# A tail of attention moved into the steps of an LSTM loop, on one NeuronCore

## The reference

```
x_proj = einsum('btd,gd->btg', x, W_ih) + b_ih + b_hh
def step(carry, xp):                       # 6250 steps, one after the other
    h, c = carry
    i, f, g, o = split(xp + h @ W_hh.T, 4)
    c = sigmoid(f) * c + sigmoid(i) * tanh(g)
    h = sigmoid(o) * tanh(c)
lstm_out = h of all steps
logits = einsum('bth,lh->btl', lstm_out, W_lin) + b_lin     # 2 classes
g = argmax(logits)                                          # 0 or 1 for each time step
w = g * lstm_out
inc = cumsum(w, axis=time);  prefix = inc - w;  suffix = inc[last] - inc
return 2.0 * lstm_out + prefix * fw_att + suffix * bw_att
x = x + that
```

## Time and profile before

| | |
|---|---|
| median of 3 runs | 13971.03 us |
| the profiled execution's own time | 13987.69 us |
| its span | 13985.9 us |
| PE, DVE, ACT busy, share of the span | 72%, 62%, 37% |
| DVE, fin of the recurrence | 13822.7 us |

### The profile page before, as it was taken

The page is one execution under the profiler, slowest core; times in us unless marked ns, Lnnn a source line. Parts: engine busy times, 40 slices in busy tenths (PEclk is TensorE's granted clock), DMA queues, the critical chain, the costliest instruction groups (busy, mean ns, idle before and its releaser), DMA issues. The chain is left out here.

```text
span 13985.9 us, 721250 instructions
## 1 busy us (share of the span) xinstructions
PE 10063.6 (72%) x285273; PEld 9131.5 (65%) x285273; DVE 8604.1 (62%) x65379; ACT 5184.4 (37%) x32393; POOL 2070.5 (15%) x1598
## 2 busy tenths in 40 slices
PE   3444444687777777777777777777777777777776
PEld 2333333567777777777777777777777777777775
DVE  4444222256666666666666666666666666666667
ACT  1111111144444444444444444444444444444443
POOL 5888788400000000000000000000000000000000
PEclk8666777865555555555555555555555555555556
DMA  6555455410000000000000000000000000000001
GB/s 164 91 90 90 80 83 83 92 34 1 1 1 1 1 1 1 1 1 1 1 1 1 1 1 1 1 1 1 1 1 1 1 1 1 1 1 1 1 1 19
DMA packets 2057504, 301.47 MB, mean 22 GB/s; under 512 B 1894943, under 2 KB 2013747, under 8 KB 2056843
## 3 DMA queue, kind: packets, MB, share of 16 engines
q0 software_dynamic: 150048, 204.90, 9.0%
q1 hardware_dynamic: 1896678, 91.09, 8.1%
q10 hardware_dynamic: 10742, 5.06, 0.1%
HBM read 153.07 MB, written 141.27 MB: 21 GB/s over the span
## 5 line engine op out<-in xcount | busy, mean ns | idle before, releaser
L1422 PE MATMUL bank<-hp,whh 128*128 128x1 f16 (+1 forms) x225000 | 7000.0, 166 | 2320.7 <-DVE hp L1553 2320.7
L1422 PEld LDWEIGHTS bank<-hp,whh 128*128 128x128 f16 x225000 | 6488.6, 104 | 2864.1 <-DVE hp L1553 2863.6
L1500 ACT ACTIVATE gates<-last_banks 128x3 f32<-128x3 f32 x12500 | 2085.4, 174 | 6161.2 <-DVE last_banks L1538 6161.2
L1538 DVE TENSOR_REDUCE last_banks<-bank 128x3 f32<-128x6 f32 x12500 | 2076.6, 172 | 2393.9 <-PE bank L1422 2393.9
L1422 PE MATMUL bank<-xsteps,wih 128*128 128x10 f16 (+1 forms) x45036 | 2331.0, 170 | 0.0
L1542 DVE CUSTOM_DVE_ANT_1 uv<-gates 128x4 f32<-128x4 f32 x12500 | 2019.4, 164 | 506.3 <-ACT gates L1500 0.2
L1553 DVE TENSOR_TENSOR_SCAN hp<-last_banks,opening 128x2 f16<-128x2 f32 x12500 | 1968.9, 161 | 569.1 <-ACT last_banks L1509 108.7
L1509 ACT ACTIVATE last_banks<-gates 128x1 f32<-128x1 f32 x12500 | 2085.2, 174 | 0.1
L1422 PEld LDWEIGHTS bank<-xsteps,wih 128*128 128x128 f16 x45036 | 1917.6, 104 | 0.0
L1558 DVE TENSOR_TENSOR_SCAN hp<-last_banks,hp 128x2 f16<-128x2 f32 x12500 | 1759.2, 159 | 0.0
L1629 POOL TENSOR_TENSOR U<-U (+1 forms) x25 | 27.5, 1139 | 11171.2 <-POOLq L1572 11171.2
(11 more groups left out here) (184 smaller groups left out, 3199.8 us busy)
## 6 DMA issues: line engine op xcount, KB each, us to landing
xsteps<-x_d SPq DMA_DIRECT2D x1252, 5.0 KB, 1.8
U<-hp SPq DMA_DIRECT2D x1250, 5.0 KB, 2.5
acc_d<-zero SPq DMA_DIRECT2D x30, 640.0 KB, 12.9
ht<-acc_d SPq DMA_DIRECT2D x75, 224.0 KB
rows<-xn_d,staged_i POOLq DMA_INDIRECT x782
acc_d<-sums,target POOLq DMA_INDIRECT x782, 3.8
xi<-xn_d SPq DMA_DIRECT2D x50, 125.0 KB
xi<-in_x SPq DMA_DIRECT2D x50, 125.0 KB
```

Of the source, the lines that this page charges most:

```text
L1422: return nc.tensor.matmul(to, w, v, start=start, stop=True, skip_group_check=True)
L1500: nc.scalar.activation(gates[:, k, 0:6:2], zi[k], ACT.Tanh, scale=down)\
L1538: nc.vector.tensor_reduce(zi[k], gi[k][b][:, s], axis=AX.X, op=ALU.add).then_inc(ifg_summed[k], 1)
```

## The change

All of the attention that doesn't need the last sum is done within the recurrence, ten time steps at a time, one iteration behind. DVE gets, behind `state2` of each step, a piece of it (`join` and `follow`): step 0 joins the second half of the ten states just finished, step 1 adds twice the states to `XT`, step 3 makes the gate, step 4 weighs, step 5 joins the first half of the running iteration's states, steps 6 and 7 do the running sum of the halves `k` = 0, 1, and steps 8 and 9 add to `XT`, for `k` = 0 and 1, first the weighted states times `minus_fw`, then the running sum times `diff`; the second of the two waits on the first, through the semaphore `after`. PE gets, in steps 1 and 2, behind the step's products, two float32 matmuls each (`class_logits`: 128x128 weights `wlb`, 10 columns), and its 44 ahead matmuls are shared out anew (`share`: 12, 3, 3, 12, 14, for both groups). ACT adds the bias to the first logit at the end of step 2. The stores of the states into `U` go, with their waits. Weights and constants are loaded and made in the block before the recurrence. Behind the recurrence the last ten states are followed up without cover, and one pass is left: ACT adds `lastw`, PE turns, DVE (not ACT) copies out, SP stores.

```diff
@@ recurrence, SP
-                        for k in range(KD):
-                            sp.wait_ge(h2_ready[k], (2 * i + b + 1) * B)
-                            sp.sem_inc(sp_turn)
-                        sp.dma_start(Hs[:, bass.ds((2 * i + b) * B, B), :], h_pairs[:, b * B:(b + 1) * B, :, 1]).then_inc(h_out[b], 16)
@@ recurrence, PE
-                per_step = -(-(3 * KD * (1 + PARTS * KD) + KD * (1 + 3 * KD)) // B)
+                share = (12, 3, 3, 12, 14)
...
+                def class_logits(i, l):
+                    if l == 0:
+                        pe.wait_ge(after, AFTER * i - AFTER + 2)
+                    for k in range(KD):
+                        last = nc.tensor.matmul(logits[l], wlb[:, k, l, :], hj[:, k, :], start=k == 0, stop=k == KD - 1,
+                                                skip_group_check=True)
+                    if l:
+                        last.then_inc(l_made, 1)
...
+                    if b == 0 and due(i):
+                        if s == 0:
+                            pass
+                        elif s <= 2:
+                            class_logits(i, s - 1)
+                        elif s == 4:
+                            pe.wait_ge(after, AFTER * i - AFTER + 4)
+                    n = share[s]
@@ recurrence, ACT
+                    if b == 0 and s == 2 and due(i):
+                        first_logit(i)
+                def first_logit(i):
+                    act.wait_ge(l_made, i)
+                    nc.scalar.activation(l0[:], logits[0], ACT.Identity, bias=bl[:, 0:1]).then_inc(l0_ready, 1)
@@ recurrence, DVE
                     def state1(k):
                         dve.wait_ge(tc_ready[k], t + 1)
-                        if s == 0 and due(16 * i):
-                            dve.wait_ge(h_out[b], 16 * i)
...
+                    if b == 1 and s == 0:
+                        join(i, 0, t)
+                    elif due(i):
+                        follow(i, b * B + s, t)
+
+                def join(i, half, t):
+                    for k in range(KD):
+                        dve.wait_ge(h2_ready[k], t)
+                    at = slice(half * B, half * B + B)
+                    nc.vector.tensor_tensor(hj[:, :, at], hp[:, at, :, 2].rearrange("p t k -> p k t"),
+                                            hp[:, at, :, 3].rearrange("p t k -> p k t"), ALU.add).then_inc(after, 1)
+
+                def follow(i, at, t, last=False):
+                    first = AFTER * i - AFTER
+                    cols = bass.ds(i * (2 * B) - 2 * B, 2 * B)
+                    stt = nc.vector.scalar_tensor_tensor
+                    if at == 0:
+                        join(i, 1, t)
+                    elif at == 1:
+                        dve.wait_ge(after, first + 2)
+                        stt(out=XT[:, :, cols], in0=hj[:], scalar=2.0 / (1 << H_EXP), in1=XT[:, :, cols], ...)
+                    elif at == 3:
+                        dve.wait_ge(l0_ready, i)
+                        stt(out=gate[:], in0=logits[1], scalar=bl[:, 1:2], in1=l0[:], op0=ALU.add, op1=ALU.is_gt)...
+                    elif at == 4:
+                        dve.wait_ge(after, first + 4)
+                        nc.vector.tensor_tensor(wgt[:], hj[:], gate[:]..., ALU.mult).then_inc(after, 1)
+                    elif at in (6, 7):
+                        dve.wait_ge(after, first + 5)
+                        k = at - 6
+                        nc.vector.tensor_tensor_scan(inc[:, k, :], one[:], wgt[:, k, :], inc[:, k, 2 * B - 1:2 * B],
+                                                     ALU.mult, ALU.add).then_inc(after, 1)
+                    elif at in (8, 9):
+                        k = at - 8
+                        stt(out=XT[:, k, cols], in0=wgt[:, k, :], scalar=minus_fw[:, k:k + 1], in1=XT[:, k, cols],
+                            op0=ALU.mult, op1=ALU.add).then_inc(after, 1)
+                        dve.wait_ge(after, first + (8 if last else 9) + 2 * k)
+                        stt(out=XT[:, k, cols], in0=inc[:, k, :], scalar=diff[:, k:k + 1], in1=XT[:, k, cols],
+                            op0=ALU.mult, op1=ALU.add).then_inc(after, 1)
@@ behind the recurrence: joins, logits, choose, weigh, forward and the second pass's sums go; left are
+                    for k in range(KD):
+                        last = nc.scalar.activation(fin[:, b, k, :], XT[:, k, at], ACT.Identity, bias=lastw[:, k:k + 1])
+                    last.then_inc(fin_ready, 1)
...
+                    nc.vector.tensor_copy(ob[:, b].rearrange("p j d -> p (j d)"), bank[2 + b][0:R, :]).then_inc(ob_ready, 1)
```

More of the change, by code:

```diff
@@ L139, in gps_layer_kernel @@
         unscale = sb("unscale", [128, 1], I32)
+        wl = sb("wl", [128, KD, 2])
+        wlb = sb("wlb", [128, KD, 2, 128])
+        bl = sb("bl", [128, 2])
+        fw, bw, diff, minus_fw = (sb(n, [128, KD]) for n in ("fw", "bw", "diff", "minus_fw"))
+        one = sb("one", [128, 2 * B])
+        inc = sb("inc", [128, KD, 2 * B])
+        lastw = sb("lastw", [128, KD])
+        att_in, lastw_ready = sem("att_in"), sem("lastw_ready")
         ZW = (N + SPARE) * D // 128 // ZS
@@ L1348, in gps_layer_kernel @@
             hp = sb("hp", [128, 2 * B, KD, 4], F16, st)
-            h_pairs = hp[:].rearrange("p t k c -> p (t k c)").bitcast(F32).rearrange("p (t k c) -> p t k c", k=KD, c=2)
+            hj = sb("hj", [128, KD, 2 * B], F32, st)
+            l0 = sb("l0", [128, 2 * B], F32, st)
+            gate = sb("gate", [128, 2 * B], F32, st)
+            wgt = sb("wgt", [128, KD, 2 * B], F32, st)
+            logits = [bank[5][:, 32 + 16 * l:32 + 16 * l + 2 * B] for l in range(2)]
+            AFTER = 11
             opening = sb("opening", [128, 2], F16, st)
@@ L1369, in gps_layer_kernel @@
             ifg_act, o_act, c_ready, tc_ready = pair("ifg_act"), sem("ogate_act"), pair("c_ready"), pair("tc_ready")
-            h_out = [sem(f"h_out{b}") for b in range(2)]
+            after, l_made, l0_ready = sem("after"), sem("l_made"), sem("l0_ready")
             XW = KD * B * PARTS
@@ L1489, in _ @@
                 steps(pe, body)
+                for l in range(2):
+                    class_logits(NI, l)
             @block.scalar
@@ L1519, in _ @@
                 steps(act, body)
+                first_logit(NI)
             @block.vector
@@ L1570, in _ @@
                 steps(dve, body)
+                for at in (0, 1, 3, 4, 6, 7, 8, 9):
+                    follow(NI, at, N, last=True)
+                dve.wait_ge(after, AFTER * NI)
+                nc.vector.tensor_tensor(lastw[:], bw[:], inc[:, :, 2 * B - 1], ALU.mult).then_inc(lastw_ready, 1)
         stage.close()
         with ExitStack() as st:
-            wl = sb("wl", [128, KD, 2], F32, st)
-            wlb = sb("wlb", [128, KD, 2, 128], F32, st)
-            bl = sb("bl", [128, 2], F32, st)
@@ L1579, in gps_layer_kernel @@
[L1579 to L1587, removed]
@@ L1605, in _ @@
             def _(sp):
[L1606 to L1612, removed]
                 def body(c, n, b):
@@ L1623, in _ @@
                 sp.wait_ge(out_done[1], 32 * (NC // 2))
[L1625 to L1631, removed]
             @block.tensor
             def _(pe):
[L1635 to L1648, removed]
                 def body(c, n, b):
                     pe.wait_ge(fin_ready, c + 1)
-                    if b:
+                    if due(c - 1):
                         pe.wait_ge(ob_ready, c - 1)
-                    else:
-                        if due(c):
-                            pe.wait_ge(ob_ready, c)
                     for j in range(2):
@@ L1736, in forward @@
-                def forward(c, first=False, last=False):
-                    at = bass.ds(c * C, C)
-                    if not last:
-                        choose(c + 1)
-                    dve.wait_ge(wgt_ready, c + 1)
-                    if not first:
-                        dve.wait_ge(last_ready, c)
-                    for k in range(KD):
-                        start = 0.0 if first else last_inc[:, k:k + 1]
-                        nc.vector.tensor_tensor_scan(inc[:, k, at], one[:], wgt[:, k, :], start, ALU.mult,
-                                                     ALU.add).then_inc(scan_done, 1)
-                    for k in range(KD):
-                        stt(out=XT[:, k, at], in0=wgt[:, k, :], scalar=minus_fw[:, k:k + 1], in1=XT[:, k, at],
-                            op0=ALU.mult, op1=ALU.add).then_inc(base_ready, 1)
-                    dve.wait_ge(scan_done, 2 * c + 2)
-                    nc.vector.tensor_copy(last_inc[:].rearrange("p (k o) -> p k o", o=1),
-                                          inc[:, :, bass.ds(c * C + (C - 1), 1)]).then_inc(last_ready, 1)
-                    if not last:
-                        weigh(c + 1)
@@ L1757, in _ @@
[L1757 to L1776 removed]
+                def body(c, n, b):
+                    dve.wait_ge(fin_turned, c + 1)
+                    if due(32 * n):
```

(2 more changed lines are left out.)

113 lines of the change are left out of this document (31 added, 82 removed).

## The result

The changed kernel takes 14227.27 us (median of 4 runs, 14222.84 to 14238.61) against 13969.15 of the kernel before on the same chip (13965.97 to 13977.05): ratio 1.0185, 95% interval 1.0168 to 1.0203. It is 258 us slower; 233 were forecast. The profiled execution took 14222.84 us, 235 more than that of before; that this lies so near 233 is luck, as the part on the sum shows.

A forecast was written before the change was run, and what follows sets the result against it. No engine is full, so a chain from engine to engine was taken to bind the kernel. Loop +349 us (-0.10 + 0.36 + 0.30, x624) and ends -116 gave +233: 13971 to 14204 us, range 13960 to 14330.

The forecast's parts named there:

- The waits for the stores: DVE, step 0: without the register operation and second wait ahead of state1, 0.10 us less an iteration.
- The class logits: PE, steps 1 and 2: 0.93 us of work where 0.74 is free, 0.18 a step, +0.36 us an iteration.
- the low bound: Class logits on PE: no cost if the float32 weight loads are hidden wholly.
- the other bound: Class logits on PE: 0.30 us a step if each load and matmul takes 0.24 by changing between float32 and float16.
- DVE's pieces: DVE between state2 and the reduce: pieces fit into 0.54 us in steps 0 to 8, no added cost.
- The branch: DVE, step 9: the second update's wait holds the sequencer before the loop's branch, 0.84 instead of 0.54 us, +0.30 an iteration.
- ACT: End of step 2: first_logit's wait for the logits is covered by 0.2 us and the reduce's 0.17, no cost.
- The sum for the loop: Recurrence loop: -0.10 + 0.36 + 0.30 = +0.56 us an iteration, x624 = +349 us.
- The ends: Behind the recurrence: 47 us instead of 163, -116, with chunks of 1.5 us; block before the loop: nothing.
- The whole sum: Loop and ends together: +349 - 116 = +233 us, 14204 us against 13971.
- The clock: Granted clock: expected to stay at 0.50; the clock rival had a chance of 0.03.

The follow-up runs named there:

- experiment five: Kernel before, with DVE's waits for the stores moved behind state2 of steps 3 and 8, stores kept: 13919.51 us against 13975.17, ratio 0.9959.
- Three: Changed kernel with share = (14, 0, 0, 14, 16), so no ahead matmuls in steps 1 and 2: 14132.23 us, ratio 1.0115 to the kernel before.
- four: Changed kernel with wlb and hj in bfloat16 instead of float32: 14013.5 us, ratio 1.0029 to the kernel before.
- One: Changed kernel with XT updates spread over steps 6 to 8, none waiting on its own step, step 9 empty: 14018.41 us, ratio 1.0032 to the kernel before.
- two: As One, but the diff update of k = 1 stands in step 9, its wait already met: 14017.75 us, ratio 1.0031 to the kernel before.

## Why the prediction was right, step by step

- *The waits for the stores, -0.10 an iteration.* Right: 1.81 to 1.72 in the changed kernel, and alone in experiment five, -0.11 an iteration (17.31 to 17.20): 0.09 in step 0, the rest 0.01 at most in any other. That the loop's start and the stores were not the cause is shown by five, which keeps both; that it was the register operation and not the second wait, by step 5 of the kernel before.
- *The class logits, +0.36.* Right: +0.174 and +0.173. The price came from a row with one moving column, 0.213 a record; with ten columns the trace has the same 0.21, though a matmul record lasts 0.366 us instead of 0.349: either runs into the next load, which starts 0.21 behind it. Three showed the budget, four that the float32 type is the cause. The float32 loads were not free, the low bound: the records start 0.213 us apart (median of 300 iterations), and so does the matmul ahead behind the last of them, so the other bound, 0.24 by the change of type, didn't come either. Few columns are not the whole reason, since the bfloat16 records of experiment four have ten columns too and start 0.03 apart, with loads of 104 ns. Why a float32 record takes 0.213 stays open. The 0.01 that I took off for the start-up behind a wait was my estimate, and no run shows it by itself: they show 0.17 a step where 0.93 is 0.19 over the 0.74 that is free.
- *DVE's pieces, 0.* Right for steps 0 to 8, but in step 8 by less than I thought: an update of 10 elements takes 0.22 to 0.23 us, where I took 0.16 to 0.2, and step 8's second ends 0.02 us after the reduce starts.
- *The branch, +0.30.* Right in kind, small in size: +0.34. The mis-sized term is the updates' duration: the second starts 0.26 us behind the first (8016.50 to 8016.76), where I took 0.20 from the earlier trace rows; it starts 0.38 behind `state2` (the pair of 8016.26 ends at 8016.54, one takes 0.16), not 0.34; the rest, from there to the reduce, is 0.50 as said. That the sequencer takes up the loop's register operation at the start of the last instruction that has something to wait for is shown by the 0.01 us between the two starts, before and after. One and two, with step 8, showed that it is the wait and not the length of the loop's body, 131 instructions in all three.
- *ACT.* Right: ACT has added the bias 0.48 us before the next tanh can start, and steps 3 to 8 stay at 1.72.

```profile
8004.33 0.27 ACT L1570 ACTIVATE l<-bank,bl 128x10 f32<-128x10 f32 x1 [0.39 <-PE bank L1469]
8005.09 0.33 ACT L1549 ACTIVATE gates<-last_banks 128x3 f32<-128x3 f32 x2 [0.48 <-DVE last_banks L1594]
```

- *The sum for the loop.* +0.58 an iteration instead of +0.56: 362 us instead of 349.
- *The ends, -116.* Measured: 49.7 us behind the recurrence (14171.41 to 14221.1) against 163.2, -113.5. A chunk takes 1.62 us (3.24 for two), not 1.5. I set the copy at 0.65 and the time to the landing at 2.3: they are 0.70 and 2.55 (14182.61 to 14185.16, with the issue).
- *The whole sum.* Loop and ends make 362 - 113.5 = +249 where +233 was forecast: 13 too little for the loop, 3 too much for the ends. The medians differ by 258; the 9 left are inside the interval of the ratio (some 24 us to each side) and aren't explained. The two profiled executions differ by 235 alone, because in that of the changed kernel the recurrence began 13.5 us earlier. So 235 beside 233 is luck. The first reduces, after and before:

```profile
2990.11 0.26 DVE L1594 TENSOR_REDUCE last_banks<-bank 128x3 f32<-128x6 f32 x2 [3.25 <-PE bank L1451]
...
3003.63 0.26 DVE L1538 TENSOR_REDUCE last_banks<-bank 128x3 f32<-128x6 f32 x2 [5.00 <-PE bank L1422]
```

  The block in front only got instructions, and in the profiled execution of experiment one, which has the same blocks, the first reduce came at 3001.23, 11 us later than this (in those of the others between 2994 and 3005). So I take it for the spread of the part ahead of the recurrence, which no experiment looked into.
- *The clock.* It stayed at 0.50, as the earlier trace rows let expect, through steps 1 and 2 and on into step 3, where PE had no idle time at all:

```profile
8000.40:8005.40 5.00, 4.98 (x131) 4.99 (x132) 3.33 (x29) 2.08 (x14) 0.00 (x0) 0.50 0.00 0
```

  Busy records did not bring more than 0.50, neither here (4.98 of 5.00 us) nor as 84% of the recurrence.

## What to carry to other kernels

Work moved into a chain's idle time was free here as long as it fitted and cost one to one from there (0.08 us less of PE's work made steps 1 and 2 0.08 shorter each), so size each piece against the idle time of its own step. Price a matmul with few columns by a row of its own type: here 0.42 us in float32, 0.03 in bfloat16. Keep an instruction that waits on the one before it away from a loop's branch where that branch has no time to spare: here the sequencer stood still with it, and the branch came on top, 0.34 us an iteration; moved to another step the same instruction cost nothing (step 9 at 1.72). The place of a wait, and of the register operation that it needs, can matter even when what it waits for costs nothing itself: 0.09 us in step 0 here, with the stores still running in experiment five.

## What the runs showed of the hardware that I had not expected

- An update (`scalar_tensor_tensor`) of 128x10 float32 takes 0.22 to 0.23 us, the running sum of 10 also 0.23, where a scan of 2 elements takes 0.16.
- An update ahead of the loop's branch whose wait was met cost nothing (experiment two): the loop's register operation started before the update did.
- The loop's body grew by 15 instructions on DVE (116 to 131), and from the branch to the first register operation it still took 0.3 us (8016.8 to 8017.1).
